# A transformer layer with routed tokens: order lists of their own, and five more PSUM banks, for the work behind the last attention scores

## The reference, cut to what matters

```python
x = L0_attn_x                                  # (16, 512, 128): 16 sequences
x = _layernorm(x + _L0_attn_ref(x, w_q, w_k, w_v, w_o))   # 16 heads of 8, q and k normed,
                                                          # tanh soft cap, causal softmax
# then, per sequence:
weights = x @ router_w + router_b              # one number for each token
topv, topi = jax.lax.top_k(weights, 64)        # the 63 above the 64th go on
x_sel = x[bidx, sel_idx]                       # 63 tokens gathered
hn = rmsnorm(x_sel, ln1)
q, kk = rope(heads(hn @ wq), pos_sel), rope(heads(hn @ wk), pos_sel)
a = softmax(q @ kk.T / sqrt(hd) + m_sel)       # 16 heads over the 63 tokens
x1 = x_sel + (a @ v) @ wo
x2 = x1 + gelu(rmsnorm(x1, ln2) @ w1) @ w2
out = zeros.at[bidx, sel_idx].set(x2 * w_sel)  # scattered back
x = _layernorm(x + out + x * (1 - sel_mask))
```

## Time and profile before

| | us |
|---|---|
| median of 3 runs | 833.04 |
| the runs | 833.2, 833.04, 830.16 |
| the profiled execution | 828.81 |
| its span, first to last instruction | 825.8 |
| last tanh of the scores ends (ACT) | 710.1 |
| PE busy, share of the span | 624.4, 76% |
| DVE busy | 596.5, 72% |
| ACT busy | 549.7, 67% |
| POOL busy | 395.6, 48% |

### The profile page before, as it was taken

How to read it: one execution, slowest core, us unless ns; L and a number is a source line. 1 busy time by engine, 2 the same in 40 slices (tenths; PEclk the granted TensorE clock), 3 DMA queues, 4 the chain that set the end, 5 groups by cost and what they waited for, 6 DMA issues and landing times.

```text
span 825.8 us, 16681 instructions
## 1 busy us (share of the span) xinstructions
PE 624.4 (76%) x6576; PEld 365.3 (44%) x6576; DVE 596.5 (72%) x1681; ACT 549.7 (67%) x403; POOL 395.6 (48%) x399
## 2 busy tenths in 40 slices
PE   3457677779778987898688978898789869865652
PEld 2223333444445454555355445544464535355232
DVE  4542827767788698968886888779896987587455
ACT  0578787778779895869766986888697978500000
POOL 5263535445733755457455664547536553511201
PEclk8577777799879997989788987899699979965755
DMA  6321303024120503030304030230303030000001
GB/s 191 64 50 29 64 15 64 14 46 136 25 53 2 129 3 76 27 66 13 77 12 80 14 64 16 59 46 5 61 27 64 2 64 28 13 1 26 0 0 51
DMA packets 96910, 36.72 MB, mean 44 GB/s; under 512 B 68018, under 2 KB 94146, under 8 KB 96834
## 3 DMA queue, kind: packets, MB, share of 16 engines
q1 hardware_dynamic: 96834, 35.67, 19.2%
...
## 4 chain that ended last, share of the span: by engine, by line
PE 46%; DVE 23%; ACT 13%; issue 12%; POOL 5%; POOLq 0%; DVEq 0%
PE ps_y L1250 15%; ACT pr L763 8%; PE ps_s L1231 5%; ACT pr L774 4%; POOL k_wide L663 4%; PE ps_a L1281 3%; PE ps_m L1281 3%; PE ps_m L1407 2%; DVE wins L989 2%; PE ps_a L1444 2%; PE ps_m L1309 2%; PE ps_a L1309 2%; PE ps_m L1257 2%; DVE v_aug L887 2%; PE ps_m L1359 1%
## 5 line engine op out<-in xcount | busy, mean ns | idle before, releaser
L763 ACT ACTIVATE pr<-ps_s 128x1024 f32<-128x1024 f32 (+1 forms) x256 | 278.0, 1128 | 121.8 <-PE ps_s L1231 81.6
L774 ACT ACTIVATE pr<-pr 128x2304 f32<-128x2304 f32 x128 | 271.6, 2122 | 1.8
L654 POOL TENSOR_TENSOR pr<-pr,tri 128x256 f32<-128x256 f32 (+2 forms) x192 | 145.6, 775 | 173.8 <-ACT pr L774 173.8
L1231 PE MATMUL ps_s<-q_st,k_st 32*64 32x512 f16 (+7 forms) x2048 | 130.2, 328 | 49.0 <-ACT pr L763 45.3
L1250 PE MATMUL ps_y<-pr,v_aug 128*32 128x512 f32 (+7 forms) x2048 | 155.8, 439 | 1.1 <-POOL pr L661 1.1
L1231 PEld LDWEIGHTS ps_s<-q_st,k_st 32*64 32x64 f16 x2048 | 52.5, 111 | 123.0 <-ACT pr L763 53.9
L675 POOL TENSOR_TENSOR st<-qk,st 128x1024 f16<-128x1024 f32 x32 | 73.9, 2328 | 35.2 <-DVE st L903 35.2
L1250 PEld LDWEIGHTS ps_y<-pr,v_aug 128*32 128x32 f32 x2048 | 57.8, 113 | 70.2 <-issue 49.9
L663 POOL TENSOR_TENSOR k_wide<-qkT,head_of 128x1024 f32<-128x1024 f32 x16 | 30.1, 1902 | 61.8 <-DVE qkT L1072 61.8
L661 POOL TENSOR_TENSOR pr<-pr,tri 128x256 f32<-128x256 f32 x64 | 54.2, 847 | 0.0
L663 POOL TENSOR_TENSOR r<-x,rw_row 128x512 f32<-128x512 f32 x16 | 18.9, 1180 | 65.5 <-DVE x L965 65.5
...
## 6 DMA issues: line engine op xcount, KB each, us to landing
...
q_st<-st SPq DMA_TRANSPOSE x16, 4.5
k_st<-st SPq DMA_TRANSPOSE x16, 4.7
```

What stands on the lines that cost most here:

```text
L654: return nc.gpsimd.tensor_tensor(buf, buf, tri[:, None, :].to_broadcast([P, blocks, 64]), ALU.mult)
L763: nc.scalar.activation(slots[:, first:first + step + 1:step, c0:c1], ps_s[:, p0:p0 + 2 * n].rearrange("p (m c) -> p m c", m=2), ACT.Tanh, ...
L774: nc.scalar.activation(slots[:, slot(n), :], slots[:, slot(n), :], ACT.Exp, scale=SOFTCAP)\
L1231: last = mm(ps_s[64 * s:64 * s + 64, col:col + S - 64 * kb], k_st[rows, k, gi // 2, 64 * kb:64 * kb + 64], q_st[rows, k, gi // 2, 64 * kb: ...
```

## The change

Behind the last scores the loop's lists are no longer used. `iterations` runs the pairs -1 to 7, then step 0 of iteration 8 for the group of scores that lags behind, with no side work, and then one flat list for each engine, `PE_LAST`, `VE_LAST`, `POOL_LAST`, `ACT_LAST`. They hold the same steps, each once, with pairs counted from 8. What each step computes is not changed, nor is what it waits for apart from banks. For the steps of these lists, `BANK_LAST` gives banks out of seven: `a`, `m` and the five of `ps_s`, and `BANK_READ_LAST` the readers to wait for; `tanh` stands for all of the 256 tanh instructions. Everything up to the last scores stays as it was. SyncE's program is untouched.

```diff
+PE_LAST = (
+    "fin.y0T/1@-1", "att.S0@-2", "route.thr/1@-2", "att.S1@-2", "pv.4/1@-1", "pv.5/1@-1", "pv.6/1@-1", "pv.7/1@-1",
+    "fin.y1T/1@-1", "att.P0@-2", "fin.yT/1@-1", "att.P1@-2", "fin.wo/1@-1", "att.PV@-2", "route.wrow/0@-1",
+    "att.oT@-2", "att.wo@-2", "route.won/0@-1", "att.h2T@-2", "att.w1@-2", "route.wrow/1@-1", "sel.gather@-1",
+    "route.won/1@-1", "late.w2@-2", "route.thr/0@-1", "sel.gather1@-1", "late.sc0@-2", "sel.ET@-1", "late.sc1@-2",
+    "sel.R@-1", "sel.hnT@-1", "sel.R1@-1", "sel.qkv@-1", "sel.R2@-1", "sel.R3@-1", "sel.qkT@-1", "route.thr/1@-1",
+    "sel.RT@-1", "sel.msel@-1", "att.S0@-1", "att.S1@-1", "att.P0@-1", "att.P1@-1", "att.PV@-1", "att.oT@-1",
+    "att.wo@-1", "att.h2T@-1", "att.w1@-1", "late.w2@-1", "late.sc0@-1", "late.sc1@-1",
+)
+VE_LAST = (
+    "late.ln@-3", "sel.msel@-2", "late.root1@-3", "late.root2@-3", "fin.y0/1@-1", "att.sc0@-2", "att.mx0@-2",
+    "att.sc1@-2", "att.mx1@-2", "fin.x1/0@-1", "route.coef/1@-2", "fin.yU1/1@-1", "att.den@-2", "fin.y1/1@-1",
+    "att.PT0@-2", "fin.yT/1@-1", "route.w/0@-1", "att.PT1@-2", "fin.res/1@-1", "fin.ln/1@-1", "fin.root1/1@-1",
+    "att.o@-2", "route.row/0@-1", "att.oT@-2", "fin.root2/1@-1", "att.x1f@-2", "att.ss@-2", "route.win/0@-1",
+    "att.root1@-2", "att.root2@-2", "att.hn@-2", "fin.x1/1@-1", "att.h2T@-2", "late.norm@-3", "att.h@-2",
+    "route.w/1@-1", "route.rank/0@-1", "route.row/1@-1", "att.hp@-2", "route.win/1@-1", "att.g@-2",
+    "route.rank/1@-1", "route.coef/0@-1", "late.proc@-2", "sel.xs@-1", "sel.ss@-1", "sel.root1@-1", "sel.root2@-1",
+    "sel.hn@-1", "late.z0@-2", "sel.ET@-1", "sel.hnT@-1", "sel.qkv@-1", "sel.R@-1", "sel.qkT@-1", "sel.RT@-1",
+    "late.z1@-2", "sel.msel@-1", "late.ln@-2", "att.sc0@-1", "att.mx0@-1", "att.sc1@-1", "att.mx1@-1",
+    "late.root1@-2", "att.den@-1", "att.PT0@-1", "att.PT1@-1", "late.root2@-2", "late.norm@-2", "att.o@-1",
+    "att.oT@-1", "att.x1f@-1", "att.ss@-1", "att.root1@-1", "att.root2@-1", "att.hn@-1", "att.h2T@-1", "att.h@-1",
+    "att.hp@-1", "att.g@-1", "late.proc@-1", "route.coef/1@-1", "late.z0@-1", "late.z1@-1", "late.ln@-1",
+    "late.root1@-1", "late.root2@-1", "late.norm@-1",
+)
+POOL_LAST = (
+    "sel.zb@-2", "route.xw/0@-1", "route.xw/1@-1", "att.hh@-2", "att.hu@-2", "att.kw@-1", "att.hh@-1", "att.hu@-1",
+    "sel.zb@-1",
+)
+ACT_LAST = (
+    "att.exp@-2", "att.tanh@-2", "att.exp@-1", "att.tanh@-1",
+)
...
+BANK_LAST = {
+    "fin.y0T/1@-1": "s4",
+    "att.S0@-2": "s0",
+    "att.S1@-2": "m",
...
+    "late.sc0@-2": "s3",
+    "sel.ET@-1": "s4",
+    "late.sc1@-2": "s2",
+    "sel.R@-1": "a",
+    "sel.hnT@-1": "s3",
+    "sel.qkv@-1": "s4",
...
+    "att.S0@-1": "s1",
+    "att.S1@-1": "s2",
+    "att.P0@-1": "s1",
+    "att.P1@-1": "m",
+    "att.PV@-1": "s3",
...
+BANK_READ_LAST = {
+    "fin.y0T/1@-1": ["tanh"],
...
+    "sel.hnT@-1": ["late.z0@-1"],
+    "sel.qkv@-1": ["sel.ET@0"],
...
+    "att.S1@-1": ["late.z1@-1"],
+    "att.P0@-1": ["att.sc0@0"],
+    "att.P1@-1": ["sel.RT@0"],
...
-        def at(use, unit=None):
-            return {"a": ps_a, "m": ps_m}[BANK[use if unit is None else f"{use}/{unit.k}"]]
+        banks = {"a": ps_a, "m": ps_m, **{f"s{i}": ps_s[:, S * i:S * i + S] for i in range(5)}}
+        def last_use(key, pair):
+            return f"{key}@{pair - PAIRS}"
+        def at(use, unit):
+            key, pair = (f"{use}/{unit.k}", unit.pair) if isinstance(unit, Batch) else (use, unit)
+            return banks[BANK_LAST.get(last_use(key, pair), BANK[key])]
...
-            for p in range(-1, PAIRS + 3):
-                body(p)
+            for p in range(-1, PAIRS):
+                body(p, range(16))
+            body(PAIRS, range(1))
+            run_side(last, table, PAIRS)
...
+                for reader in BANK_READ_LAST.get(last_use(key, pair), BANK_READ[key]):
+                    if reader == "tanh":
+                        t_.wait_ge(tanh_done, B * 16)
+                        continue
```

More of the change, by code:

```diff
@@ L300 @@
     "sel.qkv": ["fin.res/0@1", "late.z0@-1"],
+}
+BANK_LAST = {
+    "fin.y0T/1@-1": "s4",
+    "att.S0@-2": "s0",
+    "route.thr/1@-2": "a",
+    "att.S1@-2": "m",
+    "fin.y1T/1@-1": "s4",
+    "att.P0@-2": "s1",
+    "fin.yT/1@-1": "s4",
+    "att.P1@-2": "s1",
+    "fin.wo/1@-1": "m",
+    "att.PV@-2": "s1",
+    "route.wrow/0@-1": "s4",
+    "att.oT@-2": "m",
+    "att.wo@-2": "s3",
+    "route.won/0@-1": "s4",
+    "att.h2T@-2": "s0",
+    "att.w1@-2": "a",
+    "route.wrow/1@-1": "s2",
+    "sel.gather@-1": "s4",
+    "route.won/1@-1": "s2",
+    "late.w2@-2": "a",
+    "route.thr/0@-1": "s3",
+    "late.sc0@-2": "s3",
[4 more added lines that the diff above has]
+    "sel.qkv@-1": "s4",
+    "sel.qkT@-1": "s4",
+    "route.thr/1@-1": "s0",
+    "sel.RT@-1": "m",
+    "sel.msel@-1": "a",
+    "att.S0@-1": "s1",
[3 more added lines that the diff above has]
+    "att.PV@-1": "s3",
+    "att.oT@-1": "s2",
+    "att.wo@-1": "m",
+    "att.h2T@-1": "a",
+    "att.w1@-1": "s3",
+    "late.w2@-1": "s3",
+    "late.sc0@-1": "s1",
+    "late.sc1@-1": "s0",
+}
@@ new lines @@
+BANK_READ_LAST = {
+    "fin.y0T/1@-1": ["tanh"],
+    "att.S0@-2": ["tanh"],
+    "route.thr/1@-2": ["sel.qkT@0"],
+    "att.S1@-2": ["sel.msel@0"],
+    "fin.y1T/1@-1": ["fin.y0/1@0"],
+    "att.P0@-2": ["tanh"],
+    "fin.yT/1@-1": ["fin.y1/1@0"],
+    "att.P1@-2": ["att.PT0@0"],
+    "fin.wo/1@-1": ["att.sc1@-1"],
+    "att.PV@-2": ["att.PT1@0"],
+    "route.wrow/0@-1": ["fin.yT/1@0"],
+    "att.oT@-2": ["fin.res/1@1"],
+    "att.wo@-2": ["tanh"],
+    "route.won/0@-1": ["route.row/0@0"],
+    "att.h2T@-2": ["att.sc0@0"],
+    "att.w1@-2": ["route.thr/1@0"],
+    "route.wrow/1@-1": ["tanh"],
+    "sel.gather@-1": ["route.rank/0@0"],
+    "route.won/1@-1": ["route.row/1@0"],
+    "late.w2@-2": ["att.h@0"],
+    "route.thr/0@-1": ["att.x1f@-1"],
+    "late.sc0@-2": ["route.thr/0@1"],
+    "sel.ET@-1": ["sel.xs@0"],
+    "late.sc1@-2": ["route.rank/1@1"],
+    "sel.R@-1": ["late.x2@-1"],
+    "sel.hnT@-1": ["late.z0@-1"],
+    "sel.qkv@-1": ["sel.ET@0"],
+    "sel.qkT@-1": ["sel.vv1@0"],
+    "route.thr/1@-1": ["att.h2T@-1"],
+    "sel.RT@-1": ["att.oT@-1"],
+    "sel.msel@-1": ["sel.R@0"],
+    "att.S0@-1": ["att.o1@-1"],
+    "att.S1@-1": ["late.z1@-1"],
+    "att.P0@-1": ["att.sc0@0"],
+    "att.P1@-1": ["sel.RT@0"],
+    "att.PV@-1": ["sel.hnT@0"],
+    "att.oT@-1": ["att.sc1@0"],
+    "att.wo@-1": ["att.PT1@0"],
+    "att.h2T@-1": ["sel.msel@0"],
+    "att.w1@-1": ["att.o1@0"],
+    "late.w2@-1": ["att.h@0"],
+    "late.sc0@-1": ["att.PT0@0"],
+    "late.sc1@-1": ["route.thr/1@0"],
@@ L709, in _, with body @@
                      "att.hh": att_hh, "att.hu": att_hu}
-            def body(p):
-                for s in range(16):
+            def body(p, steps):
+                for s in steps:
                     g = group(p, s, 1)
@@ L1189, in _, with body @@
                         for stage in root_of for part in (1, 2)}}
-            def body(p):
-                for s in range(16):
+            def body(p, steps):
+                for s in steps:
                     for half in range(2):
-                        run_side(VE_ORDER, table, p, s, half)
-            iterations(body)
+                        run_side(VE_ORDER[2 * s + half] if p < PAIRS else (), table, p)
+            iterations(body, VE_LAST, table)
         @block.tensor
@@ L1390, in sel_msel @@
                     for c in range(NT):
-                        last = mm(at("sel.msel")[rows, 0:SLOTS], RT[:, c, rows], E[:, c, rows], start=(c == 0),
+                        last = mm(at("sel.msel", q)[rows, 0:SLOTS], RT[:, c, rows], E[:, c, rows], start=(c == 0),
                                   stop=(c == NT - 1))
@@ L1398, in sel_qkT @@
                 for s in range(2):
[L1399 removed]
+                    last = tr(at("sel.qkT", q)[:, P * s:P * s + P], qk_r[:, D * s:D * s + D], ident[:, :])
                 pe["sel"].done(last, "qkT", q)
@@ L1406, in att_scores @@
                     rows = slice(SLOTS * k, SLOTS * k + SLOTS)
-                    last = mm(at(f"att.S{h}")[rows, :], qkT[:, 0, rows],
+                    last = mm(at(f"att.S{h}", q)[rows, :], qkT[:, 0, rows],
                               k_wide[:, k, 8 * h:8 * h + 8, :].rearrange("p h s -> p (h s)"), start=True, stop=True)
@@ L1450, in late_w2 @@
                 for c in range(F // P):
-                    last = mm(at("late.w2")[:, 0:D], hu[:, P * c:P * c + P], w2_sb[:, c, :], start=(c == 0),
+                    last = mm(at("late.w2", q)[:, 0:D], hu[:, P * c:P * c + P], w2_sb[:, c, :], start=(c == 0),
                               stop=(c == F // P - 1))
@@ L1459, in late_sc @@
                 for c in range(NT):
-                    last = mm(at(f"late.sc{k}")[:, P * c:P * c + P], ET[rows, P * c:P * c + P], proc[rows, :], start=True, stop=True)
+                    last = mm(at(f"late.sc{k}", q)[:, P * c:P * c + P], ET[rows, P * c:P * c + P], proc[rows, :], start=True, stop=True)
```

96 lines of the change are left out of this document (47 added, 49 removed).

## The result

| | before | after |
|---|---|---|
| median, us | 832.73 (7 runs) | 824.71 (7 runs) |
| lowest to highest | 830.16 to 833.2 | 822.45 to 829.22 |
| the profiled execution | 828.81 | 823.54 |
| its span | 825.8 | 821.6 |
| last tanh of the scores starts | 708.65 | 713.83 |

The ratio of the times is 0.9912, 95% interval 0.9886 to 0.9938: 8.0 us faster by the medians.

A forecast was written before the change was run, and what follows sets the result against it. Behind the last scores, a chain alternating between TensorE and VectorE was taken to bound the kernel. Terms -2.15 - 5.95 - 0.9 - 0.7 - 1.25 - 0.6 + 0.3 = -11.25 gave 817.6 profiled, 821.8 forecast median, range 816.5 to 829.5.

The forecast's parts named there:

- The head: Start of VectorE's list: pair 5's `ln`, `root1`, `root2`, hidden in the wait for pair 6's `S0`; cost nothing, or 0.5 us.
- One sign of being wrong: Behind the last scores: a start of `pv` later than 721.2 would speak against the prediction.
- `x1f` to `xs`: Pair 6's `x1f` to pair 7's `xs`: 14.79 us to `g` instead of 15.23; `xs` at 759.1 instead of 761.26.
- the first half gives nothing: Rival, up to `xs`: an older pair's `norm` eats the order's gain, `xs` stays at 761.3; 823.9 us, chance 0.11.
- `xs` to `qkT`: Pair 7: TensorE's steps follow each other, its work sets the length; 9.0 us instead of 14.97, -5.95.
- `qkT` to the end: Last part: `S0` at full clock -0.9, gaps before `sc1` -0.7 and `PT1` -1.25, `x2` -0.6, `zb` +0.3.
- `norm` out of the way of `x2`: Last chain: pair 6's `norm` moves from before `x2` into the time of `PV`; -0.6 us.
- `zb` beside `g`: Pair 7's `zb` on POOL moves behind `hu`, beside `g`, slowing line 1086's subtraction; +0.3 us, 0 to 0.6.
- The clock doesn't come back: Rival: TensorE stays at 1.2 GHz from 754 to 775, `qkT` only at 774.6; 829.1 us, chance 0.18.
- Slower: Rival: clock not full before 721, low through the tail, `pv` 4.5 us longer; 834.5 us, chance 0.07.
- The prediction fails as a whole if anything before 710 moves: Sign of failure: everything before 710 us, ahead of the last scores' end, was taken as unchanged.

The follow-up runs named there:

- the kernel with the gather split: Kernel with seven banks, old order up to `proc` of pair 6, new order behind, plus the gather's first half moved ahead of `won` of the second batch: 819.37 us.
- the filled one: The kernel with the gather split, plus products of constants in TensorE's gaps from `RT` of pair 7 on: 816.85 us.
- the head alone: Kernel with seven banks, old order up to `proc` of pair 6, new behind, plus pair 5's `ln`, `root1`, `root2` first in VectorE's list: 826.17 us.
- `PV` first: The changed kernel with `PV` of pair 6 ahead of `fin.wo`, and `oT`, `wo`, `x1f` ahead of `wrow`, `root1`, `row`, as before the change: 821.92 us.

## Why the prediction was right, and where its steps were not

The sign and the range held: 824.71 against 821.8 in 816.5 to 829.5, with 8.0 us gained instead of 11.25. The tail's 1.87 missing us, by steps:

*The head.* This is the term that was mis-sized: "I cost them at nothing, and 0.5 us if the cover is too short." It cost 3.5 at `sc0`. The prediction added up durations from a stretch in which GpSimd was idle (3.91 for all) and put them beside `kw`, the masks and `zb`. They took 7.4. It had the earlier trace rows, where the same hold-up is visible as 0.97 instead of 0.68, and charged it to `g` alone. Nor was that "the one place where a `zb` ran beside it": in six earlier iterations of the same trace one did, and there the subtraction kept its 0.68 while `zb` took 1.49 or 1.50 instead of 1.04 (at 198.97 for the first of them). In those six the subtraction had begun some 0.1 us ahead of `zb` (198.87 there); in the seventh, at 720.78, `zb` had been running since 720.17. Which of the two starts first decides who pays. For a small operation the hold-up is not 0.3 but the rest of the GpSimd instruction: the addition of 721.59 ended at 722.68, where `kw` (718.89 + 3.76) ended at 722.65; line 1082 ended at 724.75, where the masks (722.61 + 2.11) ended at 724.72; line 987 ended at 726.42, where `zb` ended at 726.40. In the run that moved the three steps to where GpSimd was idle, the same twelve took 0.16 to 0.17 each, so the neighbour makes the price and not the operation. Of the 3.25 us between the forecast and the measured `yU1`, 2.35 are won back by `res` and `x1f`, which the prediction had too dear: from `yU1` to `x1f` it took 11.21 us where 13.56 was forecast. Part of that is not the order's doing: the forecast kept `PV` at the 3.46 of the earlier trace rows, and it took 1.94, as it did in the second trace of the unchanged kernel. One sign of being wrong did appear: `pv` began 13.10 behind the last tanh, and the sign's 721.2 is 12.55 in this count. `S1`, at half clock, took 1.97 and not 1.08. It cost nothing, as `yU1` waited for VectorE and not for `pv`.

*`x1f` to `xs`.* 15.72 us to `g` instead of 14.79. Three rows more than hold it: the `norm` of pair 5 that was put here took 2.95 instead of the 2.14 it was costed at, as the first of its eight pieces took 1.16 beside GpSimd's `xw` (750.76 to 751.94) and the rest 0.33 each; `win` beside GpSimd's `hu` took 1.50, where it takes 0.62 undisturbed; and line 1110 beside `hh` 0.52 instead of 0.23. Together that is 1.98, twice the 0.93 that is missing, so elsewhere in this part the order gained about 1 us. Behind `g` the forecast was right, 5.11 against 5.3, though put together otherwise: the half gather took 2.5 and not 1.95 (1.98 and 0.71, overlapping), as the halves of the whole had run partly side by side; VectorE waited 1.39 for `thr`.

Together these two make the gain of the first half 0.5 us instead of 2.15, which is nearer to the rival "the first half gives nothing" (823.9, chance 0.11) than to the forecast. Its reason was another in the main: not that VectorE had no room for the norm, but that GpSimd held up VectorE's operations, at the head and again in this `norm`. And the order as a whole loses 1.92 against the old one with seven banks. What else is in that 1.92 stays open. `PV` of pair 6 took 1.97 us in the kernel with the gather split and 3.46 in the filled one, whose code is the same up to there, and 3.46 and 1.94 in the two traces of the unchanged kernel, so the clock of this stretch differs between executions; and the two runs meant to part order from clock, the head alone and `PV` first, were both caught by it.

*`xs` to `qkT`.* -6.38 against -5.95: the step that carries the result was right, in length (8.59 against 9.0), in clock (1.00 to behind `R`) and in the pieces of `R`. Wrong was what it was put down to. The prediction said that banks alone would give 2.7 us; they give 7.43, 3.0 of it here and in the old order. It had named the wait itself, "for `z1` because of the shared bank", but its sum for the banks alone left it out: 2.38 us of TensorE's time. The Trainium skill ("PSUM — Partial Sum Buffer", Summary: rules for kernel authors) has the rule that PSUM should be read in one bank while the matmul writes another. The run with the banks alone agrees, with its 7.43 us, of which a part is clock; the rest is waits that the kernel itself makes, for a reader of a shared bank.

*`qkT` to the end.* `S0` was to be at full clock, -0.9; it was not (`S0` and `S1` together 3.48, the clock 0.50 from 780 to 782 and 0.72 over the stretch from 779 to 787), and 0.21 remained, close to its bound of 0. The gaps before `sc1` and `PT1` went as forecast, -0.60 and -1.17. `norm` out of the way of `x2` against `zb` beside `g` (0.85 instead of 0.69): -0.53 from `PT1` to the end, forecast -0.3.

*The rivals.* "The clock doesn't come back" was not in the traces of the changed kernel, but the filled kernel's trace shows it, for 5.0 us where the prediction had 6.4. That two runs of the changed kernel took 829.22 and 827.93, beside the rival's 829.1, would fit it; no trace of such a run is there. "Slower" did not come about, though its condition is real: in the second trace of the unchanged kernel `pv` ran partly at half clock and took 6.25 us instead of 4.48, with `yU1` 1.74 later and the tail 0.47 longer. "The prediction fails as a whole if anything before 710 moves" was put too hard: it moved by 5.2 us, but does so without any change.

Against the medians: the tail's -9.38 gave -8.0. The missing 1.4 is within what the main loop wanders, and no run settles it.
